# A DLRM tower on one core: turning the identity at the start, dense features earlier, loads of tile 1 in another order

## What is computed

```python
def _cin_forward(x, Ws, bs):
    x0 = x; h = x; xs = []
    for i in range(n_layers):
        z = (x0[:, :, None, :] * h[:, None, :, :]).reshape(B, F * G, E)
        y = relu(einsum('oc,bce->boe', Ws[i], z) + bs[i][None, :, None])
        if i != n_layers - 1:
            half = y.shape[1] // 2
            x_keep, h = (y[:, :half, :], y[:, half:, :])
        else:
            x_keep, h = (y, y)
        xs.append(x_keep)
    return jnp.sum(jnp.concatenate(xs, axis=1), axis=2)

z = _cin_forward(e, [W0, W1, W2], [b0, b1, b2])       # 1024 x 256
h = concatenate([z, dense_ctx], axis=1)               # 16 dense features more
h = maximum(h @ W_top1 + b_top1, 0.0)                 # 272 -> 512
h = maximum(h @ W_top2 + b_top2, 0.0)                 # 512 -> 256
y = h @ W_top3                                        # 256 -> 1
```

## Time and profile before

| | us |
|---|---|
| timed runs, median of 3 | 1074.82 |
| lowest and highest | 1073.98, 1075.13 |
| the profiled execution | 1078.64 |
| its span (first to last instruction) | 1076.8 |
| TensorE busy in it | 997.7 (93%) |
| VectorE, GpSimd busy | 824.0 (77%), 821.6 (76%) |
| ScalarE busy | 475.1 (44%) |
| DMA | 185.45 MB, mean 172 GB/s |

### The profile page before, as it was taken

One profiled execution on the slowest core, in us unless ns is written; L12 is line 12 of the kernel. 1 busy time (PEld: TensorE's weight loads), 2 busy tenths in 40 slices (PEclk: granted clock), 3 DMA queues, 4 the chain that ended last, 5 costly groups with the idle time before them and its releaser, 6 DMA issues.

```text
span 1076.8 us, 11324 instructions
## 1 busy us (share of the span) xinstructions
PE 997.7 (93%) x3089; PEld 569.0 (53%) x3089; DVE 824.0 (77%) x750; ACT 475.1 (44%) x595; POOL 821.6 (76%) x524
## 2 busy tenths in 40 slices
PE   2177899999999999999999999999999999999988
PEld 1033455555555555555555555555555555555555
DVE  4245788888778788887778777987778877888882
ACT  2132444355435444445435544444435454444453
POOL 7565779798897989797988989797979955666640
PEclk8588999999999999999999999999999999999999
DMA  7079989789987989799987988798987988889200
GB/s 156 5 167 204 204 191 204 156 192 205 200 189 159 206 193 191 168 206 201 198 187 162 206 186 188 175 204 192 203 179 170 202 197 186 188 187 215 66 1 0
DMA packets 49013, 185.45 MB, mean 172 GB/s; under 512 B 17571, under 2 KB 22179, under 8 KB 28389
## 3 DMA queue, kind: packets, MB, share of 16 engines
q1 hardware_dynamic: 40804, 183.15, 77.3%
q0 software_dynamic: 8192, 2.11, 1.8%
HBM read 182.06 MB, written 3.15 MB: 172 GB/s over the span
## 4 chain that ended last, share of the span: by engine, by line
PE 41%; POOL 24%; issue 17%; DVE 8%; ACT 4%; another core or an unknown queue 3%; DMA 1%; SPq 1%; POOLq 0%; DVEq 0%; ACTq 0%
PE y L616 26%; POOL low L499 16%; PE y L624 8%; POOL looked_up L489 8%; PE y L639 5%; DVE unsplit L1069 2%; DVE prod L1069 2%; DMA spread<-in_L_rec_W 1%; PE xT L588 1%; DVE acc_kept L1100 1%; POOL tail_parts L507 1%; ACT h L814 1%; DMA shifted<-xcols 0%; DVE low L1077 0%
## 5 line engine op out<-in xcount | busy, mean ns | idle before, releaser
L499 POOL TENSOR_TENSOR low<-unsplit,high 128x1024 fp32r<-128x1024 f32 x221 | 530.9, 2414 | 130.7 <-ACT high L828 126.2
L616 PE MATMUL y<-prod,w1T 128*128 128x512 f32 x1024 | 478.7, 596 | 7.2 <-issue 5.0
L1069 DVE TENSOR_TENSOR prod<-spread,h 128x1024 f32<-128x1024 f32 x288 | 346.5, 1213 | 72.3 <-PE y L616 59.6
L828 ACT CAST high<-unsplit 128x1024 fp32r<-128x1024 f32 x224 | 234.5, 1048 | 310.3 <-DVE unsplit L1069 300.5
L1069 DVE TENSOR_TENSOR unsplit<-spread,h 128x1024 f32<-128x1024 f32 x224 | 271.7, 1213 | 102.2 <-ACT h L814 96.8
L489 POOL DMA_INDIRECT looked_up<-in_tbl,ids_now x256 | 248.2, 970 | 65.4 <-issue 56.4
L616 PEld LDWEIGHTS y<-prod,w1T 128*128 128x128 f32 x1024 | 192.3, 191 | 169.6 <-issue 148.2
L624 PE MATMUL y<-high,w2T_high 128*128 128x512 f32 x448 | 225.3, 503 | 1.5 <-ACT high L828 1.5
L639 PE MATMUL y<-low,w2T_high 128*128 128x512 f32 x448 | 203.7, 535 | 12.4 <-POOL low L499 12.1
L624 PE MATMUL y<-high,w2T_low 128*128 128x512 f32 x448 | 177.0, 395 | 0.0
L814 ACT ACTIVATE h<-y,bias 64x512 f32<-64x512 f32 x128 | 83.4, 652 | 163.1 <-PE y L616 138.2
(11 more groups left out here) (115 smaller groups left out, 407.9 us busy)
## 6 DMA issues: line engine op xcount, KB each, us to landing
spread<-xcols SPq DMA_DIRECT2D x128, 1024.0 KB, 9.3
shifted<-xcols SPq DMA_DIRECT2D x124, 256.0 KB
shifted_tail<-xcols SPq DMA_DIRECT2D x124, 64.0 KB
looked_up<-in_tbl,ids_now POOLq DMA_INDIRECT x256
xcols<-xrows SPq DMA_DIRECT2D x32, 96.0 KB
spread<-in_L_rec_W SPq DMA_DIRECT2D x3, 512.0 KB, 4.9
spread<-in_L_rec_W SPq DMA_DIRECT2D x1, 1024.0 KB
wt<-in_W_top SPq DMA_DIRECT2D x2, 512.0 KB, 9.9
```

Of the source, the lines that this page charges most:

```text
L499: pool.tensor_tensor(low[kind][r][:, :, :], unsplit[kind][r][:, :, :], high[kind][r][:, :, :].bitcast(F32), ALU.subtract).then_inc(s_low[k ...
L616: last = pe.matmul(y[:, :], w, z[:, c, :], start=(n == 0 and c == 0), stop=(item in (LAST0, LAST1) and c == ITEM - 1))
L828: act.copy(high[kind][r][:, :, :], unsplit[kind][r][:, :, :]).then_inc(s_high[kind], 1)
L1069: dve.tensor_tensor(z, x[:, ITEM * n:ITEM * (n + 1), :], b[:, :].unsqueeze(1).to_broadcast([P, ITEM, COLS]), ALU.mult).then_inc(s_made[kin ...
```

## The change

Three things change, and nothing in the loops over the blocks:

- TensorE turns the identity into columns 0 to 127 of the bank `xT`, where nobody reads it: 8 times ahead of each of the four w2 groups, and 19 x 8 = 152 times in a loop ahead of `turn_x((0, 0))`.
- The dense features are turned (`turn_dense`) between the w1 and the w2 groups, and VectorE's subtractions (`dense_low`) stand there too.
- SyncE's list for the first tiles: after `xcols` of tile 0 only groups 0 and 1 of its spread are loaded; then come `xcols`, `shifted` and `shifted_tail` of tile 1, and then groups 2 and 3 of tile 0's spread.

```diff
+IDLE_TURNS, IDLE_LOOPS = 8, 19
...
             sp.wait_ge(s_stored, PREP_GROUPS)
-            load_factors((0, 0))
+            store_x((0, 0))
+            for g in range(GROUPS // 2):
+                load_spread((0, 0), g)
 
             sp.wait_ge(s_dense_parts, 1)
 
             sp.wait_ge(s_first, len(FIRST_ORDER))
-            load_factors((0, 1))
+            store_x((0, 1))
+            load_shifted((0, 1))
+            for g in range(GROUPS // 2, GROUPS):
+                load_spread((0, 0), g)
+            for g in range(GROUPS - 1):
+                load_spread((0, 1), g)
             load_factors((0, 2))
...
             for g in range(2 * GROUPS):
+                if g == GROUPS:
+                    turn_dense()
                 pe.wait_ge(s_ordered, g // 2 + 1)
+                if g >= GROUPS:
+                    for _ in range(IDLE_TURNS):
+                        pe.transpose(xT[:, 0:P], ident[:, :], ident[:, :])
                 turn(2 + g, GROUP, P, lambda c: w_turned[g // 2][:, P * (GROUP * (g % 2) + c):P * (GROUP * (g % 2) + c + 1)])
 
             pe.wait_ge(s_stored, PREP_GROUPS)
 
-
-            pe.wait_ge(s_dense, 16 * 2 * P // COPY)
-            for b in range(BLOCKS):
-                last = pe.transpose((y0, y1)[b // GROUP][:, P * (b % GROUP):P * (b % GROUP + 1)], dense_wide[:, b, :],
-                                    ident[:, :])
-            last.then_inc(s_denseT, 1)
+            with pe.Fori(0, IDLE_LOOPS):
+                for _ in range(IDLE_TURNS):
+                    pe.transpose(xT[:, 0:P], ident[:, :], ident[:, :])
...
             for n, home in enumerate(homes):
+                if n == 2 + GROUPS:
+                    dense_low()
```

More of the change, by code:

```diff
@@ L387, in _, with store_x @@
                 sp.dma_start(to, of.rearrange("(p a) -> p a", a=1)).then_inc(s_biases, 16)
-            def load_shifted(t):
+            def store_x(t):
                 sp.wait_ge(s_xrows, number(t) + 1)
@@ L394, in load_shifted @@
                 sp.wait_ge(s_xcols, 16 * (number(t) + 1))
+            def load_shifted(t):
                 x = xcols[number(t)]
-                if isinstance(t[0], int) and number(t) == 0:
-                    return
                 for j in range(GROUP):
@@ L420, in load_factors @@
             def load_factors(t):
+                store_x(t)
                 load_shifted(t)
-                if not isinstance(t[0], int) or number(t) >= 1:
-                    load_spread(after(t, -1), GROUPS - 1)
+                load_spread(after(t, -1), GROUPS - 1)
                 for g in range(GROUPS - 1):
@@ L561, in turn, with turn_dense @@
                 last.then_inc(s_turned, 1)
+            def turn_dense():
+                pe.wait_ge(s_dense, 16 * 2 * P // COPY)
+                for b in range(BLOCKS):
+                    last = pe.transpose((y0, y1)[b // GROUP][:, P * (b % GROUP):P * (b % GROUP + 1)], dense_wide[:, b, :],
+                                        ident[:, :])
+                last.then_inc(s_denseT, 1)
             pe.wait_ge(s_ident, 1)
@@ L980, in _, with dense_low @@
             lows = {2 + GROUPS + g: w2T_low[:, GROUP * g:GROUP * (g + 1), :] for g in range(GROUPS)}
+            def dense_low():
+                dve.wait_ge(s_dense_high, 1)
+                for lanes in (slice(COPY, 2 * COPY), slice(3 * COPY, P)):
+                    for n, bank in enumerate((y0, y1)):
+                        rows = slice(TOP1 * n, TOP1 * (n + 1))
+                        dve.tensor_tensor(dense_parts[lanes, rows], bank[lanes, :], dense_parts[lanes, rows].bitcast(F32),
+                                          ALU.subtract)
+                dve.tensor_tensor(wt_dense_parts[HALF:P, :], wt_dense[HALF:P, :], wt_dense_parts[HALF:P, :].bitcast(F32),
+                                  ALU.subtract).then_inc(s_dense_parts, 1)
             for n, home in enumerate(homes):
+                if n == 2 + GROUPS:
+                    dense_low()
                 dve.wait_ge(s_turned, n + 1)
@@ L1007, in _ @@
             dve.wait_ge(s_stored, PREP_GROUPS)
[L1009 to L1014, removed]
-            dve.tensor_tensor(wt_dense_parts[HALF:P, :], wt_dense[HALF:P, :], wt_dense_parts[HALF:P, :].bitcast(F32),
-                              ALU.subtract).then_inc(s_dense_parts, 1)
             dve.sem_inc(s_sum2, 1)
```

## The result

The change measured 1076.5 us (median of 13 runs, 1075.58 to 1078.37), the kernel before beside it 1074.05 (13 runs, 1073.37 to 1075.45). The ratio is 1.0023, 95% interval 1.0014 to 1.0031: **slower by 2.45 us**, where 3.0 us faster was forecast. It lies inside the range, and 0.2 us from the number of the second rival.

The account below looks back on a forecast made before the run. The start-up was taken as the bound, through the first `xcols` store and the transfers behind it. Terms 0 + 0 - 3.0 + 0 gave 1075.6 us profiled, 1071.8 for the median; range 1068.8 to 1078.2.

Parts of the forecast that it names:

- second rival: At the start: late completions belong to the profiled execution only, so `turn_x` ends 1.9 us later, 1076.7; chance 0.20.
- the carrying over: Whole kernel: sum made against the profiled 1078.64 us, then taken to the timed median, 1074.82, which is 3.82 less.
- The gathers were not the cause: Start, before `turn_x` at 53.70: the last of 32 gathers was issued at 44.80, so they did not delay it.
- Dense features sooner: Start: dense turns at 21.0, w2 all stored at 34.1 instead of 40.89; after the loop, `turn_x` done 3.0 us sooner.
- 32 idle turns: Ahead of the w2 groups, 4 times 8: hidden behind TensorE's waits for VectorE, 0; about 1 us if not.
- The loop: Ahead of `turn_x((0,0))`: 152 turns take 16.7 us plus 0.4 for wraps, ending at 51.2, 2.4 after `four_times`.
- I take full: Clock in the loop of 152 turns: full clock, 16.7 us, rather than half, 33.4.
- The new order: SyncE's loads, tile 1's rows ahead of half of tile 0's spread: zero, bounds -1 and +1 us.
- The hole of 2.5 us stays, one transfer earlier: DMA queue ahead of tile 1's `shifted`: SyncE's wait for the `xcols` store keeps its length under the moved loads.
- the third rival: Start: late completions stay and the loop stands behind them, 14.1 us later, 1088.9; chance 0.14.
- the fourth rival: Loop: turns don't hold the clock, so it takes 33.4 us and `turn_x` is done 14.2 later, 1089.0; chance 0.05.

Follow-up runs that it names:

- e7: Kernel before with SyncE's new order of loads and nothing else: 1077.9 us, ratio 1.0027.
- g4: The change with GpSimd's gathers held until the last w2 group is stored, run where releases were late: 1118.18 us.
- e5: Kernel before with only the dense turns, copies and subtractions moved ahead of the w2 groups, no idle turns: 1074.58 us, ratio 1.0003.
- f1: The change without its loop of 152 idle turns, run where releases came at once: 1076.9 us, ratio 1.0022.
- e3: The change without the loop of 152 turns and with SyncE's old order of loads, run with late releases: 1089.82 us, ratio 1.0101.
- g2: Kernel before with dense turns early, spread group 3 between tile 1's store and its wait, GpSimd's tail three gathers sooner; late releases: 1079.25 us, 1.0009.
- g3: Kernel before, dense turns and GpSimd's tail early; spread groups 0 and 1, tile 1's store, group 2, `shifted`, group 3; late releases: 1079.09 us, 1.0008.
- a1: The change itself, run again beside the kernel before, without late releases: 1076.65 us, ratio 1.0019.
- f2: The change with SyncE's old order of loads, loop kept, run where releases came at once: 1075.32 us, ratio 1.0007.
- d1: The change with GpSimd's first gather held until all w2 groups are stored, run where releases came at once: 1104.57 us.
- h1: The change without its loop of 152 turns, GpSimd's part of tile 0's tail three gathers sooner, no late release: 1075.14 us, ratio 0.9999.
- e2: The change with SyncE's old order of loads, loop kept, run with late releases: 1108.65 us, ratio 1.0274.
- groups 1 and 4: Two sets of follow-up kernels, each timed on one chip beside the unchanged kernel, which took 1078.79 and 1078.22 us.
- groups 2, 3 and 5: Three sets of follow-up kernels, each timed on one chip beside the unchanged kernel, which took 1074.42, 1074.52 and 1075.02 us.
- group 5: Last set of follow-up kernels, on GpSimd's early tail and on held gathers with wide matmuls; unchanged kernel 1075.02 us.
- e9: Kernel before with dense turns early and a spread group between store and wait for both tile 1's and tile 2's rows: 1077.27 us, ratio 1.0034.

## Why the prediction was wrong

**The step that failed is the carrying over.** The sum was made against a profiled execution of 1078.64 and taken to the median by subtracting 3.82 as if that were the same for both kernels. It wasn't: 50.44 and 53.70 of the earlier trace rows belong to executions with late releases, and the timed runs must have `turn_x` at about 49.1, as `e7` has. The second rival said just this, with 1.9 us later and 1076.7; it had 0.20 and should have led. What spoke for it was on the page: the profiled execution 3.82 above the median, and a late release worth 4.9. What I held against it, that nothing else in the trace is so late, speaks of neither. "The gathers were not the cause" is right only of their data: by `g4` the late releases need the gathers.

**Dense features sooner, -3.0:** right against the profile (3.15 sooner at `turn_x`, 3.06 in the time), nothing in the timed runs (`e5`, 1.0003).

**32 idle turns, 0:** not tried alone. `f1`, which has them, still starts `turn_x` at 48.78, so they are hidden where releases come at once. With late releases they are not free: `e3` has them and took 1.0101, its last late release at 62.68; `g2` and `g3` have none (and differ in SyncE's list and the tail) and took 1.0009 and 1.0008, with 51.67 and 53.48.

**The loop:** 16.79 us for 16.7 + 0.4, but 18.45 in `a1`, 18.44 in `f2` and 18.64 in `d1`. In these three the grant was 0.50 for 3.3 to 3.7 us of it, in `a1` from 35.0 to 38.4:

```profile
35.00:38.40 3.40, 3.40 (x18) 3.40 (x17) 0.00 (x0) 0.00 (x0) 2.65 (x3) 0.50 0.08 7
38.40:52.00 13.60, 13.60 (x126) 13.60 (x126) 2.34 (x7) 1.75 (x2) 8.26 (x11) 1.00 0.06 6
```

"I take full" was right for all of the loop in one of four executions; in the others half clock added 1.7 to 1.9 us. Its price, that it ends after the gathers, was right in size at the first store (1.8 from `e5` to `f2`). Its effect on the end wasn't: beside the new order it is hidden (`f1`, `a1`).

**The new order, 0 with bounds of 1:** wrong, the second failed step. It costs 2.9 us alone (1.0027), 2.0 without the loop (`f1` less `e5`) and 1.3 beside it (1.0019 less 1.0007); the last two are taken across two groups. "The hole of 2.5 us stays, one transfer earlier" took the hole as the landing alone. It is the landing and whatever tile 1's rows are late, and 4.8 us of transfers that had covered the latter were taken away. The rows' time was not worked out: it hangs on GpSimd's `tail_parts`, behind eight gathers, and on the clock behind that. The empty stretch is seen in all four executions with this order and no early tail (6.5 us in `e7`, 5.0 in `f1`, 3.5 in the profiled change, but 2.25 in `a1`, no more than before); that filling it with early rows gives the time back rests on the ratio of `h1`.

So the second rival came to the right number by a wrong way: it had the loss from the loop, and it is from the order.

**Late releases with the loop behind them** (the third rival): real, and dearer than 14 us, 30 in `e2`. It did not come up in the timed runs of the result.

**Turns and the clock:** the loop ran at a granted 1.00 throughout in the profiled change (34.0 to 50.6, above), and in `a1` the grant rose from 0.50 to 1.00 at 38.4, in the middle of the loop, with nothing but turns on TensorE, so the fourth rival is out. The rule of the Trainium skill, page "TensorE: Matmul & The Clock Gate", section "Part 4: PE-mode transpose", that turns don't count for the clock, does not hold in these traces.

## What to carry to other kernels

If a profiled execution is longer than the timed ones by more than the timed ones differ, look in it for a wait that is as long as the difference and ends on something that is over by the trace; a gain worked out from that wait may exist in the profile alone. A transfer that is moved out from behind a store takes the store's cover away: before moving it, work out when the data to be stored is ready, and put a transfer that doesn't need the store between its issue and the wait for it (0.9984 here). Where such a wait stands in several places, my reading of one kernel is to fill it where the transfer that is pushed back isn't the next thing waited for (`e9`, 1.0034).

## What the hardware showed

- In `g4` TensorE slowed from 9 us after the first of a row of gathers to 3.5 us after the end of the last: from one turn in 0.11 us to mostly one in 0.7 to 3.5. In groups 1 and 4 what it turned beside the gathers was released up to 36 us late (`e2`, drawn until 26.2, released at 62.51); in groups 2, 3 and 5 no release was late, and group 5 ran on the chip of groups 1 and 4, so it is no fixed property of a chip. The unchanged kernel took 1078.2 to 1078.8 us in the groups with it and 1074.05 to 1075.02 in the others. With the gathers held, the same groups were released at once (`g4`); what the other condition is, and whether it strikes each instruction or the work in it, stays open.
- A loop of 152 turns of the identity took 16.79, 18.45, 18.44 and 18.64 us where releases came at once. In the first the grant was 1.00 from before its start to its end, in the others 0.50 for 3.3 to 3.7 us and 1.00 for the rest; in `a1` it rose at 38.4 with turns alone and stayed up for the 13.6 us of turns that were left.
